# A chain of image operators: the first block's softmax product with 64 rows of values, its tiles paired in TensorE's column halves, and the pooled gate after it

## The chip, the core and the metric

The kernel runs on one core of a Trainium2 chip. The time is that of one execution on the device in microseconds; less is better. The engines are PE (TensorE), DVE (VectorE), ACT (ScalarE), POOL (GpSimd) and SP, which issues most of the transfers. They run beside each other and meet at semaphores.

## The reference

Four blocks are applied in turn to `x` of 4 images, 128 channels and 32 x 32 pixels (N = 1024 pixels). What the change touches is the first:

```
xr   = x.reshape(b, c, hw)
mm1  = softmax(einsum('bci,bcj->bij', xr, xr), axis=-1)     # 1024 x 1024 per image
x_conv = einsum('oc,bci->boi', w_conv, xr)                  # 64 rows
mm2  = einsum('boi,bij->boj', x_conv, mm1)
gap  = relu(einsum('oc,bcst->bost', w_gap, pooled x))       # 128 x 64 per image
out0 = einsum('bcs,bsj->bcj', gap, mm2) + x
```

The second block is an attention with 16-channel queries and keys over all 1024 pixels. The third is an attention over the 8 neighbours of each pixel and one over neighbouring channels, with a residual. The fourth projects to 16 channels, takes a two-dimensional transform, picks two directions by energy, scales the spectrum, transforms back and adds. All is float32.

## The kernel before, in words

An image lies in SBUF as 128 channels x 1024 pixels. Work goes by chunks of 128 pixels, 8 to an image. The first block of image a (steps named `split` to `x1`) runs beside the second and third block of image b = a - 1, and the end of the third and the projection of the fourth for image c = b - 1. The order of the steps is written out by hand in lists (`L0_ALL` for the first image alone, `START` and `STEADY` for the three overlapped ones, `L12_ALL` and `END` for what is left), and every engine goes through the same list, issuing its own part of each step and waiting on semaphores. `STEADY` runs twice in a loop. Then the transform follows, alone.

The steps that matter here:

- `gap` (PE, then ACT): the pooled image times the gate's weights, 64 x 128. `gate`: `w_conv` transposed times that, 128 x 128. `val0`: 8 matmuls, pixels of each chunk times `gate`, into `v0`; ACT copies it.
- `gram:i`: chunk i of the Gram matrix into one PSUM tile of 128 x 1024, as three fp32r products in two halves of 512 columns; DVE takes the negated row maximum; ACT takes exp into `e0`, a ring of RING0 = 4 chunks, with the row sums. ACT may overwrite a chunk once `e0_used` says that its `mix` is done.
- `norm0:i` (DVE): the reciprocal of the row sums times the values, into `v0n`.
- `mix:i` (PE): `v0n[i]` times `e0[i]` in float32, added up over the 8 chunks in the PSUM tile `acc0`. `x1:h` (DVE): half h of `acc0` plus x.
- `score:i`, `shift1`, `scoreT:i`, `e1h:i`, `e1l:i`, `attend:i`: the second block. DVE takes maxima of the scores, ACT exp and sums, then Ln; `shift1` is eight transposes on PE of a diagonal that DVE wrote, and `qs2` on DVE; `scoreT` gives the transposed scores, ACT takes exp, DVE splits them into a high and a low part (`e1h`, `e1l`), and `attend` is six matmuls into `acc1`. ACT's exp of chunk i waits until `e1l` of chunk i - 2 is done; `e1h` of chunk i until `attend` of chunk i - 3 is done.
- `asproj`, `near`, `shift2`, `chan`, `nearT`, `chanT`, `join`: the third block, with windows of 192 pixels. `near` ends in eight exps on ACT, then `shift2`: Ln on ACT, four short operations on DVE, the diagonal's transposes on PE.
- `qkproj`: the projections of the next image's `x1`.

Four PSUM tiles of two banks are there. `acc0` (number 3) belongs to `mix`, and to the projection of the fourth block. The others (0 and 1, printed as `tile`, and 2, printed as `acc`) are dealt to the steps by the class `Plan`: each takes the one that has been free the longest by its place in the list, and waits in `begin` until the last reader of the step that had it before has signalled (the table `LAST_READER`). Within `STEADY` as it stands before, `scoreT:2` and then `attend` use tile 2; `nearT:0` follows `near:1` in tile 0; and the next `qkproj:0` follows `nearT:0`.

## Time and profile before

| | us |
|---|---|
| median of 3 runs (lowest, highest) | 405.02 (403.21, 407.89) |
| span of the profiled execution | 403.1 |
| PE busy | 341.7 (85%) |
| DVE busy | 260.5 (65%) |
| ACT busy | 198.8 (49%) |
| POOL busy | 27.3 (7%) |

The profiled execution has no time of its own beside its span; the span is 0.1 us under the lowest run. In the rows below, an instruction has its line, engine, operation, output and inputs, and in brackets how long its engine had been idle and what ended that. The end of a matmul is modelled: matmuls are pipelined, and the distance between starts is what one costs in a row of them. The first image alone takes until about 38 us, the three overlapped ones until 264.64 us, the last second and third block until about 352 us, the transform the rest.

### The profile page before, as it was taken

The page shows a single profiled execution, that of the slowest core. Times are in us where ns is not written, and L with a number is a line of the kernel's source. Part 1 is how long each engine was busy: PE and PEld are TensorE (multiplying, and loading weights), DVE is VectorE, ACT ScalarE, POOL GpSimd, SP SyncE. Part 2 cuts the span into 40 slices and gives each one's busy share as a digit, 9 for nine tenths or more (in the row PEclk, how much of TensorE's full clock was granted, in tenths as well). Part 3 has the DMA queues.
Part 4 walks back from the last instruction along what each step waited for, and adds up shares of the span by engine and source line. Part 5 has one row for each costly group of instructions (what it writes and reads, how often), then busy time and mean ns, then how long its engine had stood idle before and what let it go on. Part 6 is the DMA issues. An engine that isn't in the chain of part 4 may idle for free. (4 is left out here: it accounts for less than half of the span.)

```text
span 403.1 us, 4422 instructions
## 1 busy us (share of the span) xinstructions
PE 341.7 (85%) x1408; PEld 237.8 (59%) x1408; DVE 260.5 (65%) x425; ACT 198.8 (49%) x351; POOL 27.3 (7%) x35
## 2 busy tenths in 40 slices
PE   3999777999998989999999899996599657597296
PEld 2853644785666847656775686672468356565162
DVE  1576777897598669876977797569397431301605
ACT  2445585646686646385685555667452433211000
POOL 3211100000021000002010000061001000100000
PEclk9999899999999699999998999996697957777579
DMA  7500000000000000000000000059600000000005
GB/s 247 188 0 2 0 1 0 2 0 0 2 0 3 0 0 2 0 0 2 0 0 0 0 0 0 0 192 411 230 2 0 0 2 0 0 0 2 1 0 208
DMA packets 5778, 15.08 MB, mean 37 GB/s; under 512 B 1294, under 2 KB 1998, under 8 KB 5762
## 3 DMA queue, kind: packets, MB, share of 16 engines
q0 software_dynamic: 2304, 8.39, 5.9%
q1 hardware_dynamic: 3458, 6.49, 4.6%
q8 instruction: 9, 0.15, 0.1%
q14 instruction: 7, 0.06, 0.0%
HBM read 12.78 MB, written 2.10 MB: 37 GB/s over the span
## 5 line engine op out<-in xcount | busy, mean ns | idle before, releaser
L373 PE MATMUL acc<-e,v0n 128*128 128x512 f32 x128 | 58.9, 595 | 0.9 <-DVE v0n L828 0.8
L659 ACT ACTIVATE e<-tile,nmax 128x1024 f32<-128x1024 f32 x22 | 24.5, 1115 | 38.8 <-DVE nmax L821 29.1
L860 DVE TENSOR_TENSOR e1l<-e,e1h 128x1024 fp32r<-128x1024 f32 x32 | 39.5, 1248 | 0.7
L373 PEld LDWEIGHTS acc<-e,v0n 128*128 128x128 f32 x128 | 23.5, 189 | 24.6 <-issue 20.1
L698 ACT ACTIVATE e<-tile 128x1024 f32<-128x1024 f32 x25 | 25.7, 1027 | 20.7 <-DVE e1l L860 13.9
L821 DVE TENSOR_REDUCE nmax<-tile 128x1 f32<-128x1024 f32 x22 | 26.9, 1222 | 11.0 <-PE tile L373 10.5
L864 DVE TENSOR_REDUCE nmax<-tile 128x1 f32<-128x1024 f32 x27 | 32.1, 1216 | 2.4 <-PE tile L373 2.4
L373 PE MATMUL tile<-ks,qs 96*128 96x512 f32 (+2 forms) x82 | 27.2, 426 | 6.1 <-ACT tile L688 4.2
L688 ACT ACTIVATE tile<-tile,nmax 128x1024 f32<-128x1024 f32 x27 | 29.4, 1087 | 3.0 <-DVE nmax L864 2.8
L857 DVE CAST e1h<-e 128x1024 fp32r<-128x1024 f32 x32 | 21.7, 687 | 3.5 <-ACT e L698 3.4
L373 PEld LDWEIGHTS tile<-ks,qs 96*128 96x128 f32 x82 | 15.3, 209 | 14.6 <-issue 8.1
L373 PE MATMUL tile<-qs,ks 96*128 96x512 f32 (+2 forms) x66 | 20.6, 404 | 1.6 <-DVE v1l L850 1.6
L373 PE MATMUL tile<-xh 128*128 128x512 f32 x44 | 21.1, 480 | 0.7 <-ACT tile L688 0.4
L373 PE MATMUL acc<-e1l,v1h 128*128 128x512 f32 x64 | 21.3, 415 | 0.2 <-DVE e1l L860 0.2
L373 PE MATMUL acc<-e1h,v1h 128*128 128x512 f32 x64 | 21.3, 416 | 0.0
L373 PE MATMUL acc<-e1h,v1l 128*128 128x512 f32 x64 | 21.0, 410 | 0.0
L1046 POOL TENSOR_TENSOR xl<-xin,xh 128x1024 fp32r<-128x1024 f32 x4 | 9.4, 2348 | 153.2 <-DVE xh L813 153.2
L373 PE MATMUL tile<-xl,xh 128*128 128x512 f32 x44 | 19.0, 432 | 0.0
L373 PE MATMUL tile<-xh,xl 128*128 128x512 f32 x44 | 18.8, 426 | 0.0
L373 PE MATMUL acc<-winT,x3s 128*128 128x16 f32 x64 | 15.5, 387 | 3.5 <-DVE x3s L921 3.5
L373 PEld LDWEIGHTS acc<-winT,x3s 128*128 128x128 f32 x64 | 15.5, 333 | 4.1 <-DVE x3s L921 4.1
L373 PEld LDWEIGHTS tile<-qs,ks 96*128 96x128 f32 x66 | 12.5, 195 | 5.7 <-issue 4.0
(202 smaller groups left out, 678.6 us busy)
## 6 DMA issues: line engine op xcount, KB each, us to landing
cas_h<-in_cas_h_in POOLq DMA_DIRECT2D x8, 512.0 KB, 9.6
cas_l<-in_cas_l_in POOLq DMA_DIRECT2D x8, 512.0 KB, 10.4
xin<-in_x SPq DMA_DIRECT2D x4, 512.0 KB, 4.7
out<-xin SPq DMA_DIRECT2D x3, 512.0 KB, 2.6
zexp<-in_region_in SPq DMA_DIRECT2D x2, 360.0 KB, 4.7
out<-xin SPq DMA_DIRECT2D x2, 256.0 KB, 2.4
bins<-in_bins_in SPq DMA_DIRECT2D x1, 372.0 KB, 5.1
x3s<-in_near_in SPq DMA_DIRECT2D x1, 288.0 KB, 5.6
```

The costliest lines, as they stand in the source:

```text
L373: return nc.tensor.matmul(o, lhsT, rhs, start=start, stop=stop, skip_group_check=skip)
L659: nc.scalar.activation(e0[:, i % RING0, :], t[:, :], ACT.Exp, bias=nmax0[:, i:i + 1], accum_out=sum0[:, i:i + 1]).then_inc(s["e0_ready"], 1)
L688: nc.scalar.activation(t[:, :], t[:, :], ACT.Exp, bias=nmax1[:, i:i + 1], accum_out=sum1[:, i:i + 1]).then_inc(s["sum1_ready"], 1)
L698: nc.scalar.activation(e1[:, i % STAGE, :], t[:, :], ACT.Exp).then_inc(s["e1_ready"], 1)
L821: vec.tensor_reduce(nmax0[:, i:i + 1], t[:, :], AX.X, ALU.max, negate=True).then_inc(s["nmax0_ready"], 1)
L857: vec.tensor_copy(e1h[:, i % RING, :], e1[:, i % STAGE, :]).then_inc(s["e1h_ready"], 1)
L860: vec.tensor_tensor(e1l[:, i % RING, :], e1[:, i % STAGE, :], e1h[:, i % RING, :].bitcast(F32), ALU.subtract).then_inc(s["e1l_ready"], 1)
L864: vec.tensor_reduce(nmax1[:, i:i + 1], t[:, :], AX.X, ALU.max, negate=True).then_inc(s["nmax1_ready"], 1)
L1046: gp.tensor_tensor(xl[:], xin[:, ph.a, :], xh[:].bitcast(F32), ALU.subtract).then_inc(s["xl_ready"], 1)
```

## The change

The softmax product is taken with the 64 rows of `x_conv`, as the reference writes it. `val0` no longer waits for the gate: it multiplies the pixels by `w_conv` (now a part of `rw`), 64 columns. The step `gate` is gone on PE and ACT. `mix:i` now takes the chunks 2i and 2i + 1: the even one writes rows 0 to 63 of `acc0`, the odd one rows 64 to 127, so that their weights stand in the two column halves of the array. There are 4 such steps of 4 matmuls in place of 8 of 2. `gap` is issued twice, so that `gapT` holds the gate's 64 rows in both halves of the partitions. A new step `mid` follows the last `mix`: ACT copies the two halves of `acc0` (512 columns each) to `m2`, and PE multiplies them by `gapT` (128 rows, which also adds the even and the odd sums) into one of the three dealt tiles; `x1` reads that tile. `e0_used` now counts pairs, so ACT's exp of chunks 4 and 5 waits for `mix:0`, and that of 6 and 7 for `mix:1`. The lists are rewritten with the new steps, and with them `Plan` deals the tiles in another way.

```diff
 L0_ALL = steps(
-    "split pool gap gram:0 gate gram:1 gram:2 val0 norm0:0 gram:3 norm0:1 norm0:2 gram:4 norm0:3 mix:0 "
-    "gram:5 mix:1 gram:6 norm0:4 mix:2 norm0:5 norm0:6 gram:7 mix:3 norm0:7 mix:4 mix:5 mix:6 bn mix:7 "
-    "fold x1:0 x1:1")
+    "split pool gap gram:0 gram:1 gram:2 val0 norm0:0 gram:3 norm0:1 norm0:2 gram:4 norm0:3 gram:5 mix:0 "
+    "gram:6 norm0:4 norm0:5 norm0:6 gram:7 mix:1 norm0:7 mix:2 bn mix:3 mid fold x1:0 x1:1")
...
-               "gap": ("gapT_ready", "a", 1, lambda i: 1), "gate": ("gate_ready", "a", 1, lambda i: 1),
+               "gap": ("gapT_ready", "a", 1, lambda i: 1), "mid": ("x1_ready", "a", 2, lambda i: 2),
...
-                        end(step, mm(t[0:POOL * POOL, 0:P], pooled[:], wgT[:], True, True))
-                    elif name == "gate":
...
+                        mm(t[0:SQ, 0:P], pooled[:], wgT[:], True, True)
+                        end(step, mm(t[SQ:P, 0:P], pooled[:], wgT[:], True, True))
...
-                            last = mm(t[:, cu], xs[:, cu], gate[:], True, True)
+                            last = mm(t[:, u * SQ:(u + 1) * SQ], xs[:, cu], rw[:, 3, 0:SQ], True, True)
...
-                        pe.wait_ge(s["e0_ready"], a * CH + i + 1)
-                        pe.wait_ge(s["v0n_ready"], a * CH + i + 1)
+                        pe.wait_ge(s["e0_ready"], a * CH + 2 * i + 2)
+                        pe.wait_ge(s["v0n_ready"], a * CH + 2 * i + 2)
                         if i == 0:
 
-                            wait_past(pe, s["x1_ready"], 2 * a)
+                            wait_past(pe, s["mid_ready"], 2 * a)
...
-                            last = mm(acc0[:, hc], v0n[:, i, :], e0[:, i % RING0, hc], i == 0, i == CH - 1)
+                            for odd in range(2):
+                                u = 2 * i + odd
+                                last = mm(acc0[odd * SQ:(odd + 1) * SQ, hc], v0n[:, u, :], e0[:, u % RING0, hc],
+                                          i == 0, i == CH // 2 - 1, True)
                         last.then_inc(s["e0_used"], 1)
+                    elif name == "mid":
+
+                        t = begin(step)
+                        pe.wait_ge(s["gapT_ready"], a + 1)
+                        for h in range(2):
+                            hc = slice(h * HALF, (h + 1) * HALF)
+                            pe.wait_ge(s["mid_ready"], 2 * a + h + 1)
+                            mm(t[:, hc], gapT[:], m2[:, hc], True, True).then_inc(s["mid_full"], 1)
...
+                    elif name == "mid":
+                        act.wait_ge(s["e0_used"], (a + 1) * (CH // 2))
+                        wait_past(act, s["x1_ready"], 2 * a)
+                        for h in range(2):
+                            hc = slice(h * HALF, (h + 1) * HALF)
+                            nc.scalar.activation(m2[:, hc], acc0[:, hc], ACT.Copy).then_inc(s["mid_ready"], 1)
...
-                        wait_past(act, s["e0_used"], a * CH + max(i - RING0 + 1, 0))
+                        wait_past(act, s["e0_used"], a * (CH // 2) + max((i - RING0) // 2 + 1, 0))
...
-                        dve.wait_ge(s["e0_used"], (a + 1) * CH)
-                        vec.tensor_tensor(x1[:, hc], acc0[:, hc], xin[:, a, hc], ALU.add).then_inc(s["x1_ready"], 1)
+                        dve.wait_ge(s["mid_full"], 2 * a + i + 1)
+                        t = slots[ph.slot(("mid", 0))]
+                        vec.tensor_tensor(x1[:, hc], t[:, hc], xin[:, a, hc], ALU.add).then_inc(s["x1_ready"], 1)
```

Three places in the order. First, PE ahead of `attend:0` beside the second image (`qs,ks` are `scoreT:2` and `scoreT:3`). Before:

```order
L373 MATMUL acc<-qs,ks 128x512 [waits e1_ready,qs2_ready]
L373 MATMUL acc<-qs,ks 128x512
L373 MATMUL acc<-e,v0n 128x512 [waits v0n_ready,e0_ready]
L373 MATMUL acc<-e,v0n 128x512
L373 MATMUL tile<-qs,ks 128x512 [waits e1_ready,qs2_ready]
L373 MATMUL tile<-qs,ks 128x512
```

With the change:

```order
L371 MATMUL tile<-xl,xh 128x512
L371 MATMUL tile<-xh,xl 128x512
L371 MATMUL tile<-qs,ks 128x512 [waits e1_ready,qs2_ready]
L371 MATMUL tile<-qs,ks 128x512
L371 MATMUL acc<-qs,ks 128x512 [waits e1_ready,qs2_ready]
L371 MATMUL acc<-qs,ks 128x512
L371 MATMUL tile<-xh 128x512 [waits e0_ready,xl_ready]
```

`scoreT:3` and no longer `scoreT:2` is the last to use tile 2 (`acc`) before `attend:0`, and the `mix` between them is gone.

Second, ACT after the exps of `near` (the rows of 128x192). Before:

```order
L725 ACTIVATE tile,sum<-tile,nmax 128x192 [waits nmax1_ready,tile_full0]
L725 ACTIVATE tile,sum<-tile,nmax 128x192 x3
L693 ACTIVATE log<-sum 128x8 [waits sum1_ready]
L708 ACTIVATE xkeep<-x,ngama,keep 128x1024 [waits x2_ready]
L713 ACTIVATE ec,sumc<-tile,nmaxc 128x128 [waits nmaxc_ready,tile_full1]
```

With the change:

```order
L733 ACTIVATE tile,sum<-tile,nmax 128x192 [waits nmax1_ready,tile_full1]
L733 ACTIVATE tile,sum<-tile,nmax 128x192 x3
L649 ACTIVATE m<-acc 128x512 [waits x1_ready,e0_used]
L649 ACTIVATE m<-acc 128x512
L701 ACTIVATE log<-sum 128x8 [waits sum1_ready]
L716 ACTIVATE xkeep<-x,ngama,keep 128x1024 [waits x2_ready]
L721 ACTIVATE ec,sumc<-tile,nmaxc 128x128 [waits nmaxc_ready,tile_full1]
```

The two copies of `mid` stand ahead of the Ln on which `shift2` rests.

Third, PE from `shift2` (`ident,diag`) over `chan` to `nearT:0`. Before:

```order
L472 MATMUL acc<-ident,diag 96x128 [waits e0_ready,diag_ready]
L472 MATMUL acc<-ident,diag 96x128 x7
L373 MATMUL tile<-x2T 128x128 [waits sum1_ready,masks_ready,x2T_ready]
L373 MATMUL tile<-x2T 128x128 x7
L373 MATMUL tile<-chainb,identb 128x128
L373 MATMUL tile<-nearb,identb 128x192 [waits sum1_ready,qs2_ready]
L373 MATMUL tile<-qs,ks 128x160
```

With the change:

```order
L371 MATMUL acc<-m,gapT 128x512 [waits mid_ready,gapT_ready,e0_ready]
L371 MATMUL acc<-m,gapT 128x512 [waits mid_ready]
L476 MATMUL tile<-ident,diag 96x128 [waits sum1_ready,diag_ready]
L476 MATMUL tile<-ident,diag 96x128 x7
L371 MATMUL tile<-x2T 128x128 [waits sum1_ready,masks_ready,x2T_ready]
L371 MATMUL tile<-x2T 128x128 x7
L371 MATMUL tile<-chainb,identb 128x128
L371 MATMUL acc<-nearb,identb 128x192 [waits x1_ready,qs2_ready]
L371 MATMUL acc<-qs,ks 128x160
```

`nearT:0` now stands in tile 2, which `mid` had before it, and waits for `x1_ready`, that is for both halves of `x1`. `nearT:1` is in tile 0, so that the next `qkproj:0`, in tile 0 as before, follows `nearT:1`, and waits for ACT's exp of it. On DVE the second half of `x1` stands behind the `chan` step in both kernels.

## Rows read from the trace of the kernel before

**Rows 1.** Page: PE's busy time, granted clock by slice, costliest group.

```profile
PE 341.7 (85%) x1408; PEld 237.8 (59%) x1408; DVE 260.5 (65%) x425; ACT 198.8 (49%) x351; POOL 27.3 (7%) x35
...
PEclk9999899999999699999998999996697957777579
...
L373 PE MATMUL acc<-e,v0n 128*128 128x512 f32 x128 | 58.9, 595 | 0.9 <-DVE v0n L828 0.8
```

**Rows 2.** Groups of instructions by form: count, busy us, mean ns.

```profile
L373 PE MATMUL acc<-cas_h,xp 128*128 128x512 f32 x16 | 8.0, 497 | 0.8 <-DVE xp L929 0.8
...
L373 PE MATMUL acc<-cas_l,xp 128*64 128x512 f32 x16 | 7.7, 481 | 0.0
```

**Rows 3.** Timeline (start us, us, what, idle), first image's end.

```profile
28.38 8.74 PE L373 MATMUL acc<-e,v0n 128*128 128x512 f32 x20
30.37 1.11 ACT L659 ACTIVATE e<-tile,nmax 128x1024 f32<-128x1024 f32 x1 [1.90 <-PE acc L373]
31.59 1.28 ACT L627 ACT_TABLE_LOAD   x1
35.76 0.68 DVE L792 TENSOR_SCALAR rws<-rw,scale 128x128 f32<-128x128 f32 x3
38.08 1.95 PE L373 MATMUL tile<-x,wT 128*128 128x512 f32 x4 [0.63 <-DVE x L833]
```

**Rows 4.** Timeline, scores beside the second and third image.

```profile
52.01 2.36 DVE L864 TENSOR_REDUCE nmax<-tile 128x1 f32<-128x1024 f32 x2 [1.04 <-PE tile L373]
63.91 3.96 PE L373 MATMUL acc<-e,v0n 128*128 128x512 f32 x8
67.42 0.16 DVE L879 TENSOR_TENSOR diag<-shf,shf_h 128x8 f32<-128x8 f32 x1
128.96 1.22 DVE L821 TENSOR_REDUCE nmax<-acc 128x1 f32<-128x1024 f32 x1 [0.68 <-PE acc L373]
```

**Rows 5.** Timeline, attention beside the second image.

```profile
76.79 0.63 PE L373 MATMUL acc<-e1h,v1h 128*128 128x512 f32 x2
76.97 1.03 ACT L698 ACTIVATE e<-tile 128x1024 f32<-128x1024 f32 x1 [0.84 <-DVE e1l L860]
91.23 1.88 PE L373 MATMUL acc<-e,v0n 128*128 128x512 f32 x4
92.99 1.10 PE L373 MATMUL acc<-x,wT 128*128 128x512 f32 x2
```

**Rows 6.** Timeline, windowed scores beside the second image; a half-tile copy.

```profile
100.93 5.35 PE L373 MATMUL acc<-e,v0n 128*128 128x512 f32 x12
104.92 0.21 ACT L693 ACTIVATE log<-sum 128x8 f32<-128x8 f32 x1
105.65 0.16 DVE L879 TENSOR_TENSOR diag<-shf,shf_h 128x8 f32<-128x8 f32 x1
106.11 1.04 PE L472 MATMUL acc<-ident,diag 128*96 128x128 f32 x8
...
362.32 0.60 ACT L742 ACTIVATE zneg<-acc 128x512 f32<-128x512 f32 x1 [3.09 <-PE acc L373]
```

**Rows 7.** Timeline, the turn from the second image to the third.

```profile
108.83 0.25 PE L373 MATMUL tile<-nearb,identb 128*128 128x192 bf16 x1
109.87 0.81 ACT L731 ACTIVATE e<-tile 128x768 f32<-128x768 f32 x1
110.31 0.68 DVE L833 TENSOR_TENSOR x<-acc,xin 128x512 f32<-128x512 f32 x1
110.73 0.81 ACT L731 ACTIVATE e<-acc 128x768 f32<-128x768 f32 x1
110.86 2.09 PE L373 MATMUL tile<-x,wT 128*128 128x512 f32 x4
112.18 0.69 ACT L672 ACTIVATE full<-tile,bias 128x512 f32<-128x512 f32 x1 [0.47 <-PE tile L373]
```

**Rows 8.** Timeline, transposes after a long wait of PE.

```profile
327.97 1.94 PE L472 MATMUL acc<-ident,diag 128*96 128x128 f32 x8 [4.53 <-DVE diag L879]
```

More of the change, by code:

```diff
@@ L28 @@
 POOL = 8
+SQ = POOL * POOL
 HID = C // 8
@@ L130, in __init__ @@
             age[slot], self.last[slot] = at + 3, step
-            if not accumulates:
+            if not accumulates and name != "mid":
                 self.nth[step] = self.fills[slot]
@@ L205, in conv_seq @@
         slots = (tile[0], tile[1], acc1, acc0)
-        rw = sb("rw", [P, 3, P])
+        rw = sb("rw", [P, 4, P])
         rp = sb("rp", [P, 3, 6])
@@ L211, in conv_seq @@
         wgT = sb("wgT", [P, P])
-        wc = sb("wc", [POOL * POOL, P])
         winT = sb("winT", [P, M])
@@ L251, in conv_seq @@
             xl = sb0("xl", [P, N], F32R)
-            v0 = sb0("v0", [P, CH, P])
-            v0n = sb0("v0n", [P, CH, P])
+            v0 = sb0("v0", [P, CH, SQ])
+            v0n = sb0("v0n", [P, CH, SQ])
+            m2 = sb0("m2", [P, N])
             e0 = sb0("e0", [P, RING0, N])
@@ L257, in conv_seq @@
         cas_l = sb("cas_l", [P, CH, N], F32R)
-        pooled = sb("pooled", [P, POOL * POOL])
-        gapT = sb("gapT", [POOL * POOL, P])
-        gate = sb("gate", [P, P])
+        pooled = sb("pooled", [P, SQ])
+        gapT = sb("gapT", [P, P])
         nmax0 = sb("nmax0", [P, CH])
@@ L347, in _ @@
                 if b == 0:
-                    for dst, src in ((ident, ident_in), (wgT, wg_t), (wc, w_conv), (rp, rows_p), (rw, rows_w),
+                    for dst, src in ((ident, ident_in), (wgT, wg_t), (rp, rows_p), (rw, rows_w),
                                      (sc, scal)):
@@ L403, in _ @@
                         if isinstance(a, int) and a == 0:
-                            pe.wait_ge(s["weights_in"], 16 * 6)
+                            pe.wait_ge(s["weights_in"], 16 * 5)
                         t = begin(step)
-                        end(step, mm(t[0:POOL * POOL, 0:P], pooled[:], wgT[:], True, True))
-                    elif name == "gate":
-                        pe.wait_ge(s["gapT_ready"], a + 1)
-                        t = begin(step)
-                        end(step, mm(t[:, 0:P], wc[:], gapT[:], True, True))
+                        mm(t[0:SQ, 0:P], pooled[:], wgT[:], True, True)
+                        end(step, mm(t[SQ:P, 0:P], pooled[:], wgT[:], True, True))
                     elif name == "val0":
-                        pe.wait_ge(s["gate_ready"], a + 1)
                         pe.wait_ge(s["xs_ready"], a + 1)
@@ L635, in _ @@
                         t = take(step)
-                        nc.scalar.activation(gapT[:], t[0:POOL * POOL, 0:P], ACT.Relu,
-                                             scale=float(POOL * POOL) / N).then_inc(s["gapT_ready"], 1)
-                    elif name == "gate":
-                        t = take(step)
-                        nc.scalar.activation(gate[:], t[:, 0:P], ACT.Copy).then_inc(s["gate_ready"], 1)
+                        wait_past(act, s["x1_ready"], 2 * a)
+                        nc.scalar.activation(gapT[:], t[:, 0:P], ACT.Relu,
+                                             scale=float(SQ) / N).then_inc(s["gapT_ready"], 1)
+                    elif name == "mid":
+                        act.wait_ge(s["e0_used"], (a + 1) * (CH // 2))
+                        wait_past(act, s["x1_ready"], 2 * a)
+                        for h in range(2):
+                            hc = slice(h * HALF, (h + 1) * HALF)
+                            nc.scalar.activation(m2[:, hc], acc0[:, hc], ACT.Copy).then_inc(s["mid_ready"], 1)
                     elif name == "split":
@@ L765, in fold_bn @@
                 par = [rp[:, :, i] for i in range(6)]
-                dve.wait_ge(s["weights_in"], 16 * 6)
+                dve.wait_ge(s["weights_in"], 16 * 5)
                 vec.tensor_scalar(var[:], par[4], EPS, None, ALU.add).then_inc(s["small_dve"], 1)
@@ L810, in _ @@
                             dve.wait_ge(s["x_rest_in"], 16 * (B - 1))
-                            dve.wait_ge(s["e0_used"], a * CH)
+                            dve.wait_ge(s["e0_used"], a * (CH // 2))
                         xa = xin[:, a, :]
@@ L1027, in constants @@
             def constants():
-                pool.wait_ge(s["weights_in"], 16 * 6)
+                pool.wait_ge(s["weights_in"], 16 * 5)
                 pool.wait_ge(s["const_in"], 16 * 3)
@@ L1132, in _pack @@
     f = np.float32
-    rows_w, rows_p = np.zeros((P, 3, P), f), np.zeros((P, 3, 6), f)
+    rows_w, rows_p = np.zeros((P, 4, P), f), np.zeros((P, 3, 6), f)
+    rows_w[:, 3, 0:SQ] = i["L0_conv_w_conv"].T
     rows_w[:, V] = i["L1_conv_v_w"]
```

4 lines of the change are left out of this document (2 added, 2 removed), and 15 rows, old and new, of the table STEADY.

## The prediction

> **What bounds the kernel now.** I read the page first. PE is busy for 85% of the span, DVE for 65%, and the costliest group of all is the softmax product that the change halves [rows 1]. That alone would say: less PE work, less time. So I went to the timeline of PE, DVE and ACT side by side, to see where PE is late and where it only fills a wait. The reader is to see three kinds of stretch. In the last 8.74 us of the first image's PE row, the product runs in one block [rows 3]. In the attention stretch, PE starts `attend:0` at 76.79 and has no gap until 91.23 [rows 5]: PE bounds there. In the score stretches, in the eight exps and after them, PE waits for DVE and ACT, and the product lies in those waits. The 12 matmul rows that start at 100.93 end at about 106.1, but `shift2`, which starts at 106.11, could not have started before 105.8, because the diagonal that it transposes was written at 105.65 [rows 6]. The rows from 63.91 end at 67.7, the diagonal there is written at 67.58 [rows 4].
>
> **What the product costs.** 20 rows take 8.74 us, the last one 0.6: 0.43 us from start to start [rows 3]. A matmul of the program makes two rows. 128 rows [rows 1] are 54.7 us.
>
> **The pairing.** If an even and an odd matmul run at once, a step of two chunks (8 rows) costs 4 x 0.43 = 1.7 us, or 2.1 if the first and the last row have no partner; if not, 3.4. No row shows matmuls in different column halves. What a row shows is that half a width by itself is no cheaper: 481 ns beside 497 [rows 2]. So the bounds are 1.7 and 3.4 for each step; I take 2.1, since the two write different rows and have weights of their own, and keep 3.4 as a rival. The Trainium skill (TensorEngine Tiling (Array Packing), Theoretical Speedup) gives up to 2x for a dimension of at most 64, which is the lower bound; (TensorE: Matmul & The Clock Gate, Measured speedup vs the span model) has 2.38x for three column tiles, by which I estimate 1.6x for two and 2.15 us for a step. No run here shows either yet.
>
> PE's whole account, were it the bound everywhere: 54.7 becomes 27.4, `mid` adds 2 matmuls of two rows to each image, 1.7 us, 6.8 in all, and the gate's 8 rows and the doubled `gap` nearly cancel: 20.5 us less. Now by place.
>
> **A, first image: -1.2.** ACT's exp of chunks 4 and 5 waits for `mix:0`, and that of 6 and 7 for `mix:1`, which PE's list has behind `gram:7`. Walking the list with the durations of the rows (gram 1.36 us of PE, maximum 1.22 of DVE, exp 1.3 of ACT) I get `mix:0` at 20 to 22, exp 4 until 23.3, `mix:1` at 24.7 to 26.6, exp 6 until 27.9 and exp 7 until 30.85, against 31.5 now [rows 3]. The fold of the second block's weights follows it (table loads from 31.59, `rws` done at 36.44, `qkproj` at 38.08), so 0.7 is gained, and another 0.5 as PE no longer reaches the fold late, at 36.96. `mid` is hidden by that fold. Ends: -2.3 if `mix:1` holds nothing up, +0.3.
>
> **B, scores: -1.1, -0.3, -0.3.** The gate's matmul and copy go, and the copy of `v0` is half as long, about 0.4 less of ACT. DVE's waits there, 1.04 in the second image and 0.68 in the third [rows 4], bound what they were worth. `mix:0` stays beside `shift1`'s diagonal and costs nothing; at 3.4 it would cost 1.5.
>
> **C, attention: +1.3 in each of three images.** Taking a `mix` out ahead of `attend:0` frees nothing: the Gram step behind it waited for an exp anyway. But tile 2 now goes from `scoreT:3` to `attend:0`, so `attend:0` waits for the fourth exp, which starts at 76.97 and takes 1.03: 78.05 in place of 76.79 [rows 5]. PE is without a gap from there to the end of the stretch, so 1.3 us arrives there whole. Nothing excludes it but DVE's own lateness, which is smaller (`e1h:3` waits for `attend:0`, about 1.0). Sum 3.9.
>
> **D, `mix:1` on the path: +0.5 each.** Before, one chunk, 1.7 us, lies between the last `attend` and `asproj` (91.23, 92.99) [rows 5]. Now a pair lies there: 2.1 less 1.7 is 0.4 (bounds 0 and 1.7). ACT's exp 6 now waits for that pair and stands ahead of the first copy of `asproj`, which it holds 0.3 longer. Together 0.7 with a pair of 2.1, and 0.3 with one of 1.7; I take 0.5, 1.5 for three. The Trainium skill (TensorEngine Tiling (Array Packing), Key Properties) says that changing the tiling mode drains TensorE, a rule against short tiled steps between full ones, as here; it gives no figure, and no run here shows one yet.
>
> **E, `mid` ahead of `shift2`: +1.1 each.** The eight exps end at 104.9 [rows 6], counted without the shift of C and D. PE is done with the pairs by then, at 104.4. ACT copies two halves, 0.60 each by the nearest row [rows 6], to 106.15; only then come Ln and the short chain to the diagonal, 0.9 as before, and `shift2` starts at 107.2 in place of 106.11. `mid` on PE (105.5 to 107.2) ends at the same time. Ends: 0.5 if the copies overlap the exps, 1.5. Sum 3.3.
>
> **F, the turn to the next image: +2.8 each.** Now `nearT:0` runs at 108.83, before `x1` has its second half (110.31 to 110.99) [rows 7]. With the change it sits in `mid`'s tile and waits for that half: 111.0. It takes 0.86 (the two of them and a transpose fill 108.83 to 110.86), so its exp on ACT goes from 112.05 to 112.9 and the second from there to 113.7 (0.81 each [rows 7]). `qkproj:0` waits for the second, as its tile was `nearT:1`'s: 113.7 in place of 110.86. ACT's copy `full`, at 112.18, and all of the next image's scores hang on it, so 2.8 is on the path. It holds for three turns: 8.4. Ends: 2.4 and 3.2.
>
> **Sum.** -1.2 - 1.7 + 3.9 + 1.5 + 3.3 + 8.4 = +14.2 on the profiled span of 403.1: 417.3. The median of the runs shown is 1.9 above that span, so I say 419. The transform at the end is not touched.
>
> **What is not in the sum.** PE waits more around each turn. Where it waits long its clock is lower: the granted clock is 0.9 to 1.0 in most slices and 0.5 to 0.7 late in the page [rows 1], between the levels of 1.2 and 2.4 GHz. The eight transposes take 1.04 at 106.11 [rows 6] and 1.94 after a wait of 4.53 [rows 8]. If a turn ran at the low level, its four projection rows and the next would cost some 2 to 3 us more: up to 9 in all.
>
> **Rivals.**
> 1. The halves do not run at once. Steps cost 3.4: then A becomes +2.4 (each of the two held exps comes 1.7 later), B adds 1.5 per image, D 1.3, E 3.0 (`mid` waits for the second pair). 14.2 + 3.6 + 3 x 5.8 = 35.2: 440. For it: half a width alone costs full time [rows 2], and no row shows overlap. Against: the two halves share nothing in PSUM rows or weights.
> 2. PE is the bound after all: the waits of C, E and F are made up, since the list before them runs ahead by what PE saves. Its place is the stretch from `shift1` to `nearT`; its price is the 20.5 us, of which half is 10: 395. It decides if PE's saving puts it more than 5 us per image ahead of the exps of `near`. For it: 85% busy. Against: those exps depend on `attend:7`, and C has that later.
> 3. The tile waits of F cost half, because DVE and ACT have other work queued there (the next image's cast and pooling), and A and B give 2 more each: 14.2 - 4.2 - 4 = +6 or less, 405 to 411.
>
> **Numbers.** Forecast as summed, with or without a slow clock, 412 to 428: 0.66. Rival 1, 440: 0.12. Rival 2, 395: 0.11. Rival 3: 0.11, of which 0.07 lies within 1% of 405. One per cent, 4 us, is about what a measurement of this kernel can tell, as its runs spread over 4.7. So faster 0.12, same 0.07, slower 0.81. The range 409 to 432 leaves out rivals 1 and 2.
>
> **What would show it.** Right: `attend:0` starts just as the fourth exp ends; two copies of 0.6 ahead of Ln; PE idle for 2 us before `nearT:0`, released by DVE's `x1`; `qkproj:0` released by ACT's second exp of `nearT`. The paired rows start 0.2 us apart on average. Wrong: pairs at 0.43 apart (rival 1), PE without those waits (rival 2). The forecast fails most easily at F, since it is 8.4 of 14.2.

## The result and the profile after

The changed kernel is slower: 440.18 us median of 4 runs (435.79 to 441.74) beside 405.51 (403.21 to 407.89) for the kernel before, a ratio of 1.0832 with a 95% interval of [1.0762, 1.0903]. The forecast was 419, in a range of 409 to 432. The sign was right, the size was not: 21 us are missing. In the experiments one, four, seven and eight some runs lie more than 1.5% above the fastest of their kernel; for these four the time given is the median of the other runs, and the upper ones stand beside it.

The profiled execution has a span of 438.8, 35.7 more than that of before. Its page, against [rows 1]: PE's busy time and clock, and the costliest group (count, then busy us and mean ns of one, then PE's idle time ahead of them).

```profile
PE 344.7 (79%) x1424; PEld 235.5 (54%) x1424; DVE 257.7 (59%) x425; ACT 200.3 (46%) x355; POOL 27.1 (6%) x35
PEclk9999888998988689989996789897668686858569
L371 PE MATMUL acc<-e,v0n 128*64 128x512 f32 x128 | 39.1, 753 | 10.4 <-DVE v0n L836 8.2
```

The product's busy time fell from 58.9 to 39.1, so the pairing works; yet PE as a whole is busy for 3 us more than before: `mid` adds 7.9, and the other rows became longer by some 15. The clock row has 8, 7 and 6 in the part of the images, where before it was nearly all 9, and PE now waits 10.4 us ahead of the product.

**Where the 35.7 us lie.** The steps that the prediction speaks of cut an image into four stretches, read off PE's timeline: from `qkproj` to the transposes of `shift1`, to `asproj`, to the transposes of `shift2`, to the next `qkproj`. In us, for the three overlapped images:

| | before | after | more |
|---|---|---|---|
| first image, to `qkproj` | 38.08 | 38.07 | 0 |
| scores (B) | 29.62, 34.06, 33.24 | 31.24, 38.05, 35.48 | 7.9 |
| attention (C, D) | 25.29, 25.24, 25.27 | 26.96, 27.02, 28.45 | 6.6 |
| windows (E) | 13.12, 13.10, 13.11 | 15.95, 15.78, 15.91 | 8.3 |
| turn (F) | 4.75, 5.05, 4.71 | 7.78, 7.80, 8.68 | 9.8 |
| last stage and transform | 138.5 | 141.6 | 3.1 |

**First image**, PE's and DVE's timeline (start, us, engine, line, operation, and in brackets how long the engine had been idle and what ended that), against [rows 3]:

```profile
31.06 3.32 PE L371 MATMUL acc<-e,v0n 128*64 128x512 f32 x8 [3.15 <-DVE v0n L836]
34.60 0.68 DVE L800 TENSOR_SCALAR rws<-rw,scale 128x128 f32<-128x128 f32 x3
35.16 1.96 PE L371 MATMUL tile<-m,gapT 128*128 128x512 f32 x4 [0.78 <-ACT m L649]
36.95 0.49 PE L396 MATMUL acc<-ident,rws 128*128 128x128 f32 x3
```

The folded weights `rws` are begun 1.16 earlier than the 35.76 of before, as forecast. But PE is then busy with `mid` and comes to the fold at 36.95, when it came to it before at 36.96.

**Scores**, second image, against the rows from 63.91 of [rows 4]:

```profile
64.41 1.11 ACT L667 ACTIVATE e<-tile,nmax 128x1024 f32<-128x1024 f32 x1 [0.44 <-issue]
65.56 0.25 DVE L836 TENSOR_SCALAR v0n<-v,rec 128x64 f32<-128x64 f32 x1
65.91 3.46 PE L371 MATMUL acc<-e,v0n 128*64 128x512 f32 x8 [2.23 <-ACT e L667]
67.51 0.17 DVE L888 TENSOR_TENSOR diag<-shf,shf_h 128x8 f32<-128x8 f32 x1
69.31 1.08 PE L476 MATMUL tile<-ident,diag 128*96 128x128 f32 x8
```

The diagonal is there at 67.7, as before. `mix:0` holds it up: it waits for both of its chunks, PE is idle for 2.23, and then its 8 rows take 3.46 where the same 8 take 1.94 in the next fence. The eight transposes start at 69.31 and not at 67.70.

**Attention**, against [rows 5]:

```profile
78.62 1.02 ACT L706 ACTIVATE e<-acc 128x1024 f32<-128x1024 f32 x1 [0.83 <-DVE e1l L869]
79.79 0.70 PE L371 MATMUL acc<-e1h,v1h 128*128 128x512 f32 x2 [1.20 <-ACT e L706]
94.40 1.94 PE L371 MATMUL acc<-e,v0n 128*64 128x512 f32 x8
96.27 1.12 PE L371 MATMUL acc<-x,wT 128*128 128x512 f32 x2
```

`attend:0` waits 1.20 for the fourth exp, as forecast for C. The pair of `mix:1` takes 1.87 from its start to the next row's.

**Windows**, against [rows 6]; the first row is that of the kernel before, at the same step as the second:

```profile
99.24 0.24 PE L373 MATMUL tile<-nearb,identb 128*128 128x192 bf16 x1 [0.32 <-issue]
102.64 0.24 PE L371 MATMUL tile<-nearb,identb 128*128 128x192 bf16 x1 [2.12 <-DVE qs L854]
105.44 4.19 PE L371 MATMUL acc<-e,v0n 128*64 128x512 f32 x16
107.81 0.42 ACT L733 ACTIVATE tile<-tile,nmax 128x192 f32<-128x192 f32 x1
109.69 1.08 ACT L649 ACTIVATE m<-acc 128x512 f32<-128x512 f32 x2 [1.34 <-PE acc L371]
110.66 0.21 ACT L701 ACTIVATE log<-sum 128x8 f32<-128x8 f32 x1
112.22 1.04 PE L476 MATMUL tile<-ident,diag 128*96 128x128 f32 x8
```

The copies of `acc0` do stand ahead of Ln and take 1.08. But they also wait 1.34 for the product: PE had been idle for 2.12 ahead of `near`, and the rows that follow are slow. This is not a wait for a tile. From the start of `asproj` to `near` it takes 6.37 us in the changed kernel and 6.25 in the one before, but with 20 rows of PE in place of 24: the `mix` of four rows that stood there is gone from that place, and PE's idle time grew from 0.32 to 2.12.

**Turn**, against [rows 7]:

```profile
116.41 0.68 DVE L842 TENSOR_TENSOR x<-acc,xin 128x512 f32<-128x512 f32 x1
117.24 0.24 PE L371 MATMUL acc<-nearb,identb 128*128 128x192 bf16 x1 [2.15 <-DVE x L842]
119.14 0.81 ACT L739 ACTIVATE e<-tile 128x768 f32<-128x768 f32 x1
120.00 3.60 PE L371 MATMUL tile<-x,wT 128*128 128x512 f32 x4 [0.79 <-ACT e L739]
```

Both waits of F are there: `nearT:0` for the second half of `x1`, `qkproj` for ACT's second exp. The four rows of `qkproj` take 3.60; before they took 2.09.

**The clock** of those places. Stretches of after, then of before (start:end and length, busy time of PE, PEld, DVE, ACT, POOL, then the granted clock as a share of 2.4 GHz; 0.5 is 1.2 GHz):

```profile
66.00:70.00 4.00, 4.00 (x14) 1.44 (x15) 0.59 (x4) 0.96 (x3) 0.00 (x0) 0.62 0.00 0
102.60:112.20 9.60, 8.77 (x36) 4.52 (x37) 4.01 (x9) 6.77 (x22) 0.00 (x0) 0.82 0.01 2
120.00:128.50 8.50, 8.50 (x32) 5.17 (x32) 4.29 (x8) 5.58 (x9) 0.25 (x1) 0.80 0.00 0
```

```profile
64.00:68.00 4.00, 3.88 (x12) 1.51 (x11) 2.31 (x8) 2.88 (x7) 0.00 (x0) 1.00 0.00 0
99.20:106.10 6.90, 6.86 (x28) 3.92 (x29) 3.85 (x9) 5.59 (x20) 0.00 (x0) 1.00 0.01 2
110.90:117.80 6.90, 6.90 (x31) 4.45 (x31) 6.49 (x10) 6.26 (x10) 2.36 (x1) 1.00 0.00 0
```

The kernel before has 1.00 at all three. The theory to test is: the sum of waits was right, and what is missing is a clock that the waits pull down. Rivals: PE's work in another form (the pairing, the copies, the early second product) is what costs; or one of the waits alone costs all of it.

### The profile page after: what moved, and what is told of

It is laid out like the page before. It is cut to its first block and busy times, and to the rows that moved or that the text cites. A ratio compares the mean times of both kernels' runs of the same rounds, so it can differ in the third digit from the quotient of the medians.

```text
span 438.8 us, 4457 instructions
## 1 busy us (share of the span) xinstructions
PE 344.7 (79%) x1424; PEld 235.5 (54%) x1424; DVE 257.7 (59%) x425; ACT 200.3 (46%) x355; POOL 27.1 (6%) x35
## 5 line engine op out<-in xcount | busy, mean ns | idle before, releaser
L371 PE MATMUL acc<-e,v0n 128*64 128x512 f32 x128 | 39.1, 753 | 10.4 <-DVE v0n L836 8.2
L667 ACT ACTIVATE e<-tile,nmax 128x1024 f32<-128x1024 f32 x20 | 22.3, 1114 | 36.7 <-PE acc L371 21.1
L829 DVE TENSOR_REDUCE nmax<-tile 128x1 f32<-128x1024 f32 x20 | 24.4, 1222 | 9.7 <-PE tile L371 9.1
L696 ACT ACTIVATE tile<-tile,nmax 128x1024 f32<-128x1024 f32 x21 | 22.8, 1087 | 8.3 <-DVE nmax L873 8.3
L371 PEld LDWEIGHTS acc<-e,v0n 128*64 128x64 f32 x128 | 10.3, 168 | 30.2 <-issue 23.2
L873 DVE TENSOR_REDUCE nmax<-tile 128x1 f32<-128x1024 f32 x21 | 25.4, 1217 | 1.2 <-PE tile L371 1.2
L371 PE MATMUL acc<-e1h,v1h 128*128 128x512 f32 x64 | 22.6, 437 | 2.8 <-ACT e L706 2.8
L371 PE MATMUL tile<-xh 128*128 128x512 f32 x40 | 18.8, 469 | 5.7 <-ACT e L667 5.1
L667 ACT ACTIVATE e<-acc,nmax 128x1024 f32<-128x1024 f32 x12 | 13.4, 1114 | 20.9 <-DVE nmax L829 15.3
L371 PEld LDWEIGHTS tile<-ks,qs 96*128 96x128 f32 x70 | 16.5, 252 | 11.4 <-issue 7.8
L850 DVE CAST qs<-full 64x512 fp32r<-64x512 f32 x16 | 7.5, 471 | 20.7 <-ACT full L680 20.6
L371 PE MATMUL tile<-nearb,identb 128*128 128x192 bf16 x44 | 12.4, 303 | 9.3 <-DVE qs L854 6.1
```

What stands on the lines that cost most here:

```text
L371: return nc.tensor.matmul(o, lhsT, rhs, start=start, stop=stop, skip_group_check=skip)
L667: nc.scalar.activation(e0[:, i % RING0, :], t[:, :], ACT.Exp, bias=nmax0[:, i:i + 1], accum_out=sum0[:, i:i + 1]).then_inc(s["e0_ready"], 1)
L696: nc.scalar.activation(t[:, :], t[:, :], ACT.Exp, bias=nmax1[:, i:i + 1], accum_out=sum1[:, i:i + 1]).then_inc(s["sum1_ready"], 1)
L829: vec.tensor_reduce(nmax0[:, i:i + 1], t[:, :], AX.X, ALU.max, negate=True).then_inc(s["nmax0_ready"], 1)
L850: vec.tensor_copy(qs[0:2 * G, hc], full[0:2 * G, hc]).then_inc(s["qhi_ready"], 1)
L873: vec.tensor_reduce(nmax1[:, i:i + 1], t[:, :], AX.X, ALU.max, negate=True).then_inc(s["nmax1_ready"], 1)
```

## The experiments

**One: the tile of `attend:0` put back.** The changed kernel, with `Plan` told to deal `scoreT:2` tile 2 and `scoreT:3` tile 1.

```diff
+FORCE = {('scoreT', 2): 2, ('scoreT', 3): 1}
 ...
+                slot = FORCE.get(step, slot) if ("gram", 4) in schedule and ("score", 0) in schedule else slot
```

> The changed kernel, with scoreT:2 dealt tile 2 and scoreT:3 tile 1, so that attend:0 waits for the third exp again and not for the fourth. Nothing else moves. If the wait for the fourth exp is on the path (term C, 1.35 us at attend:0 beside the second image), each of the three images gets 1.3 us back: 440.2 becomes about 436. If PE's clock and not this wait sets that stretch, the time stays at 440 and attend:0 starts as late as now.

Measured: 427.6 (425.98 and 429.20; two more runs 434.76 and 435.61), span 427.4. The attention stretch is 25.58, 25.58 and 25.54. Against the first two images of the changed kernel (26.96, 27.02) C cost 1.4 (forecast 1.3), and 0.3 is left for D (forecast 0.5). Three times 1.4 would be 4.2, as in the expected 436; the span fell by 11.4. Of that 5.7 lie in the attention stretches, 3.0 in the windows and 1.7 in the scores, where nothing was edited.

**Two: the tiles of the turn put back.** The same with `FORCE = {('nearT', 0): 0, ('nearT', 1): 1, ('chanT', 0): 2}`.

> The changed kernel, with nearT:0 dealt tile 0, nearT:1 tile 1 and chanT tile 2, so that nearT:0 no longer waits for x1 and the next qkproj:0 waits for the first exp of nearT only. If the turn costs what the trace shows (term F, 3.0, 2.8 and 4.0 us in the three images), it gives 8 to 10 us back: about 431. If the time there only moves to the next wait (DVE's x1, chanT behind x1:1), it gives back under 3 us: above 437. A third reading is that the idle 2.15 us also lowered PE's clock for qkproj (3.60 us against 2.09); then it gives 10 to 13: 427 to 430.

Measured: 417.56 (416.77 to 421.45), ratio to the kernel before 1.0314 [1.0254, 1.0375], span 415.3. One choice of tiles is worth 22.6 us, though the turn itself shrank by 2.3, 2.0 and 3.2 (to 5.47, 5.77 and 5.43). The other 15 came back elsewhere: the scores of the second to fourth image fell to 30.09, 33.50 and 33.44, the last stage and transform from 141.6 to 134.9, without an edit there. PE's timeline at `mix:0` and at `qkproj`:

```profile
66.26 1.94 PE L375 MATMUL acc<-e,v0n 128*64 128x512 f32 x8 [1.72 <-ACT e L671]
116.60 1.98 PE L375 MATMUL tile<-x,wT 128*128 128x512 f32 x4
```

Both run at full speed. All three readings were too high, the nearest (wait and clock together, 427 to 430) by 10: they had been put together for the turn and `qkproj` alone.

**Three: half the product, without the change.** The kernel before, with the product taken for the first 512 columns only; the second half of the product is left out and `x1` adds the first half twice.

```diff
                         for h in range(2):
                             hc = slice(h * HALF, (h + 1) * HALF)
+                            if h:
+                                continue
                             last = mm(acc0[:, hc], v0n[:, i, :], e0[:, i % RING0, hc], i == 0, i == CH - 1)
```

> The kernel before, in which each step of the softmax product is taken for the first 512 of 1024 columns only, and x1 adds that half twice; the second half of the product is left out. PE has 27 us less to do, in the same order and with the same waits. If PE's product only fills waits (as the prediction says), the time stays within 399 to 408. If PE is the bound (rival 2), it falls to 380 to 390. If the product in the waits also keeps PE's clock up, the time may even rise above 408, with a mean granted clock well under 0.90.

Measured: 408.03 (406.67 to 409.95), ratio 1.0048 [1.0019, 1.0076]. The product's group on this kernel, and the page's row of PE:

```profile
L373 PE MATMUL acc<-e,v0n 128*128 128x512 f32 x64 | 31.8, 602 | 4.9 <-DVE v0n L830 4.9
PE 324.3 (80%) x1344; PEld 231.1 (57%) x1344; DVE 258.7 (64%) x425; ACT 199.0 (49%) x351; POOL 27.3 (7%) x35
```

27.1 us of that group are gone and 17 us of PE's busy time, and the kernel is not faster: the third reading, with the lower clock (0.877, against 0.901 of the kernel before), is the one that came. The first image ends 2.3 earlier (35.74), but each turn is 1.7 longer (6.45, 6.73, 6.39). PE now waits ahead of `shift2`, and the 16 rows of `chan` behind it are slow; the third row is that of the kernel before:

```profile
104.33 1.33 PE L474 MATMUL acc<-ident,diag 128*96 128x128 f32 x8 [2.12 <-DVE diag L881]
105.45 3.37 PE L373 MATMUL tile<-x2T 128*128 128x128 f32 x16
106.99 1.95 PE L373 MATMUL tile<-x2T 128*128 128x128 f32 x16
```

So taking product off PE is worth at most the 2.3 of the first image, and three times 1.7 of clock go against it.

**Four: more work for PE.** The changed kernel, with matmuls whose results are thrown away (fillers): 9 ahead of `mix:0`, 8 ahead of `near:0`, before the waits of those steps.

```diff
+                            if ph.b is not None:
+                                for _ in range(9):
+                                    mm(acc0[:, 0:HALF], xh[:, 0:P], xh[:, 0:HALF], True, True)
                         pe.wait_ge(s["e0_ready"], a * CH + 2 * i + 2)
```

> The changed kernel with matmuls whose results are thrown away put into two of PE's waits: 9 fp32r ones (2 us) ahead of mix:0, 8 (1.8 us) ahead of near:0. If the missing time is the clock, which falls to the low level because PE idles there (mix:0 takes 3.46 us at the low level against 1.94 at the high one; near and the two mixes behind it lose about 2.5), the mean granted clock rises from 0.847 to about 0.89 and the time falls by 2 to 4 us per image: 428 to 434. If the waits alone cost the time and the clock does not matter, more PE work changes nothing or costs: 440 to 445.

Measured: 426.8 (426.25 to 427.70; one more run 434.55), ratio 1.0523 [1.0484, 1.0563], mean granted clock of the profiled execution 0.891 (0.847 without the edit). PE has 51 rows more to do and the kernel is 13 us faster, somewhat more than forecast, with the tile waits, the copies and the places of all steps as in the changed kernel. `mix:0` takes 1.94 again:

```profile
65.89 1.94 PE L371 MATMUL acc<-e,v0n 128*64 128x512 f32 x8
67.76 1.08 PE L479 MATMUL tile<-ident,diag 128*96 128x128 f32 x8
```

The windows' stretch is now 14.46, 14.26 and 14.27, which is 1.2 above before (1.3 in the first). That is the size that E was given (1.1, for the two copies); the 1.5 on top of it in the changed kernel was clock.

**Five: both choices of tiles put back.**

> The change with both tile choices of before (fourth score transpose in tile 1 so that attend:0 finds tile 2 free; nearT:0, nearT:1 and chanT out of mid's tile). Theory: the two waits and the low clock that follows them are nearly all of the 35. Alone they gave back 8 and 23, so together 31 at most: 409; if part of it was the same microseconds (the clock), 414. Rival: mid ahead of shift2 and the second wait of the pair steps hold most of what is left, and something new takes the place of one of the two: 418 or more. qkproj of the three later images should start at about 114, 194 and 274.

Measured: 415.40 (412.09 to 415.50), ratio 1.0264 [1.0221, 1.0306]. It lies between the two ranges: of the 35 of the two alone (12.6 and 22.6) 25 are there, so the two shared some of the same microseconds. Neither of the two waits is all of the 34.7. Stretches: scores 29.46, 33.57, 32.94; attention 27.12, 25.56, 25.57; windows 16.02, 14.26, 14.27; turn 5.46, 5.77, 5.44. In the first of the three images attention and windows are 1.6 and 1.8 longer than in the others, though their steps are the same: parts of them run at a granted clock of 0.76 and 0.81 (from 75 to 82 us, from 103 to 112).

**Six: `mid` after `shift2`** in the list of the three overlapped images, on top of five.

```diff
-    "gram:7 near:0 near:1 mix:2 norm0:7 mix:3 mid shift2 x1:0 xkeep chan nearT:0 nearT:1 x1:1 chanT")
+    "gram:7 near:0 near:1 mix:2 norm0:7 mix:3 shift2 mid x1:0 xkeep chan nearT:0 nearT:1 x1:1 chanT")
```

> As the kernel with both tile choices, and the product mid after shift2 in PE's and ACT's lists of the three steady stages (a shift step comes first). Theory: term E is 2.7 us per image in the changed kernel; with mid later the two copies of 0.6 us no longer stand between the exps and Ln, so 1.0 to 1.5 us per image come back, 3 to 4.5 in all: 406 to 409. Rival: the turn waits for mid instead, since x1 needs it, and nearT's exps only move: no change against the kernel with both tile choices (within 1).

Measured: 419.54 (415.61 to 421.84), a miss: slower than without this edit (415.40). In its profiled execution the windows' stretch is that of the kernel before (13.01, 12.96, 13.33), but the turn has grown to 7.24, 7.53 and 7.16, as `mid` now takes 1.7 of PE between `shift2` and `nearT`. PE's timeline:

```profile
105.95 1.08 PE L480 MATMUL tile<-ident,diag 128*96 128x128 f32 x8 [1.21 <-DVE diag L892]
106.86 1.88 PE L375 MATMUL acc<-m,gapT 128*128 128x512 f32 x4
```

So the rival was right: `mid` only moved. Windows and turn together are 20.03 and 19.71 in the later two images of five and 20.49 in both here; only the first image, where five had a low clock, gains 1.2. And the clock adds to it: the same scores stretch takes 33.03 beside the third image and 36.31 beside the fourth, and the last stage and transform take 139.15 (five: 134.75). The two scores stretches in this one execution, by their windows:

```profile
113.00:146.00 33.00, 28.71 (x129) 20.75 (x128) 26.01 (x37) 22.62 (x39) 3.38 (x2) 0.95 0.00 1
192.00:229.00 37.00, 32.84 (x132) 23.82 (x133) 26.02 (x37) 22.56 (x39) 3.39 (x2) 0.82 0.00 0
```

DVE and ACT have the same work in both; PE's rows, three more in the longer window, take 4.1 longer.

**Seven: six, with the thrown-away matmuls of four.**

> As the kernel with mid after shift2, and thrown-away matmuls on PE in its two longest waits of an image: 9 ahead of the first pair step, 8 ahead of the first near. They compute nothing that is used. Theory (the clock is part of the price, and PE's own work is not the bound): another 3 to 6 us less than without them, 401 to 405, so level with the kernel before or just below it. Rival (the clock is paid for by the tile choices already): no gain, or 1 to 3 us more as the fillers end late: 407 to 411.

Measured: 412.6 (412.54 and 412.63; two more runs 420.39 and 421.66), 8 above the range. The gain over six is 7 by the medians and 3.0 by the two profiled spans (413.8 and 410.8), so its size is not well known. The profiled execution shows the images in order (scores 29.59, 32.75, 33.01; attention 25.54, 25.58, 25.55; windows 13.01, 12.96, 12.96). Besides the 0.3 of D only the turn (7.22, 7.52, 7.16) and the last stage and transform (139.8) are longer than before.

**Eight: no pairing.** Kernel five, with the odd chunks added into the same 64 rows of `acc0` as the even ones, and `mid` over 64 rows.

```diff
-                                last = mm(acc0[odd * SQ:(odd + 1) * SQ, hc], v0n[:, u, :], e0[:, u % RING0, hc],
-                                          i == 0, i == CH // 2 - 1, True)
+                                last = mm(acc0[0:SQ, hc], v0n[:, u, :], e0[:, u % RING0, hc],
+                                          u == 0, u == CH - 1, True)
```

> As the kernel with both tile choices, but without pairing: odd chunks add into the same 64 columns as even ones, so a step of 8 rows takes 3.4 us in place of 1.9, and mid contracts 64 rows. Theory (PE waits at most places, but not in the stretch from attend:0 to asproj, nor at the last stage): a step of 1.5 more lies on the path once or twice per image, 5 to 12 us more than with pairing: 415 to 424. Rival (the product only fills waits, and more PE work keeps the clock up): within 2 us of the kernel with both tile choices.

Measured: 433.9 (431.66 and 436.17; two more runs 444.68 and 444.87), ratio 1.0719 [1.0633, 1.0806]: both expectations are too low. `mix:0`, unpaired (`mix:1` takes 3.65):

```profile
70.81 3.62 PE L375 MATMUL acc<-e,v0n 128*64 128x512 f32 x8 [1.72 <-ACT e L671]
```

So a step of 8 rows costs 3.6 unpaired and 1.94 paired, and the pairing is worth 18 us to the kernel of five. The profiled execution is one of the two long ones (span 442.9), so its stretches are upper bounds: the scores are 2.5 to 3.3 longer than in five, attention 1.7 to 3.3, windows 3.4 to 6.7. More work for PE is of no use where the path goes through it.

**Nine: the channel Gram ahead of `shift2`, on PE alone.** On top of seven: PE waited 1.21 for the diagonal there.

```diff
+                todo = list(ph.schedule)
+                if ("chan", 0) in ph.schedule and ("shift2", 0) in ph.schedule and ("mid", 0) in ph.schedule:
+                    todo.remove(("chan", 0))
+                    todo.insert(todo.index(("shift2", 0)), ("chan", 0))
```

> As the kernel with mid after shift2 and the thrown-away matmuls; in PE's list alone the channel Gram (chan, 1.95 us) also comes before shift2, where PE waited 1.2 us for DVE's diagonal. Theory (mid's 1.9 us on PE between shift2 and nearT is what remains of the turn's growth, 7.2 us from shift2 to qkproj in place of 4.75): nearT:0 can start when qs2 is there, 1.0 us earlier, shift2 starts 0.6 later; 0.5 to 1.0 per image less, 414 to 415. Rival (the copies of mid on ACT and x1 on DVE set qkproj): no change, 416 to 417.

Measured: 411.14 (410.49 to 411.60), ratio 1.0130 [1.0077, 1.0182], 1.4 less than seven, and the best of the changed kernel so far without work at its end. The turn is 5.44, 5.66 and 5.32, the windows 14.10, 13.90 and 13.90, so the two together are 0.7, 0.9 and 0.9 shorter than in seven (19.54, 19.56 and 19.22, against 20.23, 20.48 and 20.12). That is 2.5 us, as forecast; the profiled spans differ by 1.2 (410.8 and 409.6), since the first image ends at 40.11 here and at 38.14 in seven, with `mid` at the low clock.

**Ten and eleven: the kernel before, with work for PE at its end.** From 322 to the end the kernel before runs at about 0.72 of the clock. Thrown-away matmuls are put into PE's waits there, and nothing of the change: 8 ahead of `shift1` and 10 ahead of `shift2` of the last stage, 7 ahead of the last `xproj`, 12 ahead of the transpose of `sel`, 6 ahead of the second transform.

```diff
+                        if a is None:
+                            t = begin(step)
+                            for _ in range(8 if name == "shift1" else 10):
+                                mm(t[:, 0:HALF], qs[:, 0:P], ks[:, 0:HALF], True, True)
 ...
+            for _ in range(12):
+                mm(tile[0][:, 0:HALF], cas_h[:, 0, 0:P], cas_h[:, 0, 0:HALF], True, True)
```

> The kernel before, with thrown-away matmuls in PE's waits of the last stage and the transform: 8 ahead of shift1, 10 ahead of shift2, 7 ahead of the last projection of the spectrum, 12 ahead of the transpose of sel and 6 ahead of the second transform. Nothing of the change is in it. Theory (PE's waits lower its clock, and work that nobody needs can hold it up): rows that start 0.43 apart after those waits start 0.22 apart: 14 rows of the second transform 2.9 us, the two shifts 0.9 each, the spectrum's projection 1.9; 4 to 7 us less, 398 to 402. Rival (the low clock of that part is not due to the waits, since its mean is 0.76 even where PE is busy): within 1 us, or later by the fillers that outlast the wait.

Measured: 397.32 (395.22 to 398.87), ratio 0.9798 [0.9752, 0.9843]: 8 us faster than the kernel before, and the fastest of all here. The windows of the same three stretches (second and third block from `near` on, first transform, the rest), of the kernel before and of this one:

```profile
322.00:347.30 25.30, 15.16 (x80) 12.83 (x78) 8.36 (x16) 9.45 (x26) 0.00 (x0) 0.73 0.00 1
347.30:371.00 23.70, 20.29 (x68) 15.16 (x68) 1.73 (x11) 2.69 (x5) 1.04 (x1) 0.72 0.00 0
371.00:403.10 32.10, 20.83 (x81) 12.28 (x81) 13.70 (x39) 1.78 (x4) 0.00 (x0) 0.71 0.17 66
```

```profile
321.00:342.40 21.40, 16.73 (x100) 13.57 (x98) 8.36 (x16) 9.46 (x26) 0.03 (x1) 0.92 0.00 1
342.40:365.00 22.60, 19.26 (x68) 14.56 (x68) 1.71 (x11) 2.70 (x5) 1.01 (x1) 0.75 0.00 1
365.00:394.40 29.40, 23.65 (x99) 14.60 (x99) 13.73 (x40) 1.78 (x4) 0.00 (x0) 0.90 0.18 72
```

DVE's and ACT's work is the same to 0.03 us. The eight transposes of the last `shift2` [rows 8] now take 1.08:

```profile
327.17 1.08 PE L477 MATMUL acc<-ident,diag 128*96 128x128 f32 x8 [0.62 <-DVE diag L891]
```

The second kernel also moves the channel Gram ahead of `shift2` in the last stage.

> As the kernel before with thrown-away matmuls at its end, and in the last stage PE does the channel Gram ahead of shift2, where it waits for the diagonal (4.5 us). Theory: the Gram of 2 us lay between shift2 and nearT, next to DVE's 1.9 us of qs2, so at most 0.5 to 1 us less than without it. Rival: the filler and the Gram together outlast the wait and shift2 comes later: 1 us more.

Measured: 399.86 (399.09 to 400.99), ratio 0.9859 [0.9818, 0.9899]. The rival was right in sign, with 2.5 more than without it, but not in its reason: `shift2` starts at the same place (327.41, against 327.17). With the Gram moved away, PE waits 1.31 for DVE's `qs` between `shift2` and `nearT`, and the rows that follow are slow: from 327 to 342 the granted clock is 0.66, against 1.00 without this edit, and the next projection (of `x3s`) starts at 345.98 in place of 342.36.

**Twelve: everything together.** The changed kernel nine, with the fillers at the end and the channel Gram early in the last stage too.

> The changed kernel with all edits: both tile choices, mid after shift2, the channel Gram early, thrown-away matmuls in the images and in the last stage and the transform. Theory: gains add, 4 to 7 less than the same without the fillers at the end: 408 to 411, still above the kernel before, by mid's place on the path of each turn (some 1.5 us per image) and the first pair step. Rival: the clock is lost elsewhere again, no more than 2 less.

Measured: 404.84 (403.59 to 409.20), ratio 0.9989 [0.9952, 1.0027]. That is 6.3 less than nine, as forecast for the difference, and level with the kernel before, but 7.5 above the kernel before with the same fillers at its end.

## Why the prediction was wrong

The places and the mechanisms were nearly all right; the step that failed is the one in "What is not in the sum": the clock was priced at up to 9 us and left out of the sum, and the runs leave some 20 for it. Where a stretch ran at the full clock in some run, it can be set against its term, per image:

| term | forecast | measured at full clock | in the changed kernel |
|---|---|---|---|
| A, first image | -1.2 | -0.4 (four; with a lower clock it ends at 37.8 to 38.1, or at 40.1 in five) | 0 |
| B, scores | -1.1, -0.3, -0.3 | 0, -1.3, -0.2 (seven) | +1.6, +4.0, +2.2 |
| C, `attend:0` | +1.3 | +1.4 (two against one) | +1.7, +1.8, +3.2 with D |
| D, `mix:1` | +0.5 | +0.3 (one, seven) | see C |
| E, `mid` ahead | +1.1 | +1.2 (four, later images of five) | +2.8, +2.7, +2.8 |
| F, the turn | +2.8 | +2.3 by its tiles (after against two), +0.7 left | +3.0, +2.8, +4.0 |
| last stage and transform | 0 | not seen at full clock | +3.1 |

The second column sums to 14.2, the third to about 16: -0.4 - 1.5 + 4.2 + 0.9 + 3.6 + 9.0 = 15.8, with nothing for the last stage. On the span of 403.1 that is 419. The changed kernel's span is 438.8. The 19.9 between them I put down to PE rows at 1.2 GHz in place of 2.4 and what waited for them. It is a remainder and was not measured as such, but parts of it can be seen. Four gives back 4.6 of it in the windows by work for PE alone. And the last stage and transform, whose rows nobody edited, differ between the runs. Their stretch in the changed kernel and in five:

```profile
297.17:438.80 141.63, 103.80 (x391) 74.29 (x391) 64.44 (x117) 42.39 (x77) 7.62 (x12) 0.74 0.19 70
275.55:410.30 134.75, 97.99 (x391) 69.88 (x391) 64.42 (x117) 42.85 (x78) 10.98 (x18) 0.78 0.22 78
```

The same 391 rows keep PE busy for 5.8 longer, DVE's work is the same, and the stretch is 6.9 longer.

- **What is not in the sum: wrong.** It named the clock and priced it at up to 9, as four projection rows and the next at each of three turns; some 20 is what the runs leave for it. Three things were missed. The waits come back as low clock at other places, above all at `mix:0` (3.46 in place of 1.94), at `near` with the 16 product rows, and in `qkproj` (3.60 in place of 2.09). A slow row makes the next engine late, which makes PE wait again: the 1.34 that ACT's copies waited. And the product taken away makes waits of its own: ahead of `near` PE's idle time went from 0.32 to 2.12 with no new tile wait. The range should have been built with the clock in it, on all of the places where PE waits once half of the product is gone. The evidence was in [rows 8] and in the digits of [rows 1]. Four shows it from one side (more work for PE, 13 us back), two from the other (2.0 to 3.2 per turn taken out, 22.6 back).
- **A: wrong, small.** Its mechanism is there (`rws` 1.16 earlier), but "`mid` is hidden by that fold" is not so: `mid` stands ahead of the fold on PE and takes what was gained (at the full clock 0.4 is left).
- **B: right in sum at full clock, wrong in cause.** That "`mix:0` stays beside `shift1`'s diagonal and costs nothing" holds for 8 rows in 1.94, and fails for 3.46. That a step now waits for two `norm0` had not been looked at: PE's wait ahead of it is 2.23.
- **C, D, F: right.** These are the waits that were forecast with their releasers, and each is in the trace. D was 0.3 and not 0.5. Of F, 0.7 per turn stays when its tiles are put back: a part is `nearT:1`, which in tile 1 waits for ACT's exp of `chan`; the rest was not followed up.
- **E: right at full clock.** What it left out is that the product ends later than the exps, once `near` is slow: it had PE done at 104.4, and the 16 rows end at 109.6.
- **The pairing: right.** 2.1 was taken for a step, 1.94 was measured, 1.87 from start to start, near the lower bound of 1.7. The Trainium skill (TensorEngine Tiling (Array Packing), Key Properties) says that a change of the tiling mode drains TensorE. The rows agree with a small price at most: 1.87 is 0.15 above four distances of 0.43, with a paired step that stands between steps of the full array.
- **Rival 1** gave 440, which is the time that was measured, by a mechanism that isn't there: its paired rows were to start 0.43 apart. Its sum has a slip, too: two exps that come 1.7 later each make A +2.2 and not +2.4. Eight is a kernel with unpaired steps and without the two waits for tiles, and it needs 434. That the changed kernel stands at rival 1's number is chance. A number that fits says nothing for its mechanism.
- **Rival 2** (PE is the bound) is false: three takes 27 us of product off PE and gains nothing as a whole, 2.3 in the first image.
- **Rival 3** is false: F cost 3.0 and not 1.4.

What stays open: the clock's share in each stretch is a difference of stretches, in single profiled executions. The clock itself fell at other places from one stretch or execution to the next, with the same steps (in six 33.03 and 36.31 for the same stretch; the first image ends at 38.0 in two and at 40.1 in five, and from 28 to 41 us the granted clock is 0.87 and 0.74; it is 1.00 in four, which ends it at 37.7). The scatter of all runs of one, six, seven and eight (10, 6, 9 and 13 us, against 5 before) is of this size, and it goes with the clock: seven took 412.5 and 412.6 at a mean granted clock of 0.895, and 420.4 and 421.7 at 0.868 and 0.869. Why the clock falls in one execution and not in another was not found. Nor was it followed up where the 7.5 us lie that twelve is above ten.

The Trainium skill (TensorE: Matmul & The Clock Gate, What's actually happening) puts the ramp penalty, for modeling, at less than 1% of a typical kernel's span. Here the clock falls again and again within the kernel, and by the table that is worth an estimated 19.9 of 438.8, 4.5%, on top of what it costs the kernel before. The figure for one ramp would have misled here.

## What to carry to other kernels

In a kernel whose engines wait for each other, ask first which waits the work taken from TensorE had filled; here it was worth next to nothing by itself. A wait of TensorE that is new or longer can have a second price, its clock, which here was paid at rows that nobody edited. Put that price into the sum for every place where TensorE waits after the change, and look at the dealing of buffers after a list is rewritten: one choice of tiles was 22.6 of the 34.7 us here. Where TensorE must wait for microseconds at a low clock, thrown-away matmuls that end before the wait does are a cheap trial: they took the kernel before from 405.7 to 397.3. Moving work that is needed from one wait into another is not the same: in eleven it opened a new wait and lost 2.5.

## What had not been expected of the hardware

- Two matmuls in the two column halves of the array do run at once in float32: 16 rows in 3.65 us (four), where unpaired ones take 3.6 for 8 (eight).
- Fewer columns of the moving operand didn't make `val0` faster. Its 16 rows have 64 columns now, and 128 before. One of before is 275 ns in the mean, one of after 276.
- Taking work from TensorE in the middle of an undisturbed kernel (three) lowered its granted clock from 0.901 to 0.877, and in all of its runs (0.873 to 0.885, against 0.893 to 0.905).
